# A long-convolution layer on one core: sequences side by side in the spectra's rows, inverse transforms in pairs, and a new order of the engines in the last stage

## The reference, cut to what matters

```
proj = (layernorm(x) @ in_proj_w + in_proj_b).reshape(B, L, C, 3)
v = short_conv(proj[..., 0]) + short_b
h = (gelu(gelu(pos @ fw1 + fb1) @ fw2 + fb2) @ fw3 + fb3)[..., 1]
conv = irfft(rfft(v, 2 * L) * rfft(h, 2 * L), 2 * L)[:, :L]
x = x + (proj[..., 2] * conv) @ out_w + out_b
x = x + layernorm(x) @ (sum_k weights[k] * W[ids[k]]).T + sum_k weights[k] * b[ids[k]]
```

## Time and profile before

| what | value |
|---|---|
| time, median of 3 runs | 2471.45 us (2469.3 to 2475.01) |
| time of the profiled execution | 2469.04 us |
| its span | 2467.2 us |
| PE busy | 2342.2 us, 95% of the span |
| DVE busy | 1555.0 us, 63% |
| POOL busy | 913.5 us, 37% |
| ACT busy | 845.4 us, 34% |
| DMA | 207925 packets, 496.59 MB, mean 201 GB/s |

### The profile page before, as it was taken

The page is one execution under the profiler, slowest core; times in us unless marked ns, Lnnn a source line. Parts: engine busy times, 40 slices in busy tenths (PEclk is TensorE's granted clock), DMA queues, the critical chain, the costliest instruction groups (busy, mean ns, idle before and its releaser), DMA issues. The chain is left out here.

```text
span 2467.2 us, 39561 instructions
## 1 busy us (share of the span) xinstructions
PE 2342.2 (95%) x12804; PEld 1580.8 (64%) x12804; DVE 1555.0 (63%) x2188; ACT 845.4 (34%) x1151; POOL 913.5 (37%) x1189
## 2 busy tenths in 40 slices
PE   7689999999999999779999978999999999999998
PEld 2267777877787777433333326777777777777776
DVE  5834444344444434357767757888888888888886
ACT  3334444444444444234444442222222222222222
POOL 1322222222222222000000006666666666666664
PEclk9889999999999999889999989999999999999999
DMA  5534544544454554689999987655555555555553
GB/s 181 213 98 155 199 138 165 184 177 157 140 195 145 174 169 181 253 310 339 347 333 340 346 298 246 215 171 174 175 173 173 175 173 170 170 174 175 173 176 99
DMA packets 207925, 496.59 MB, mean 201 GB/s; under 512 B 18411, under 2 KB 18732, under 8 KB 190836
## 3 DMA queue, kind: packets, MB, share of 16 engines
q1 hardware_dynamic: 153588, 395.09, 49.8%
q10 hardware_dynamic: 54272, 100.68, 11.1%
HBM read 276.27 MB, written 219.43 MB: 201 GB/s over the span
## 5 line engine op out<-in xcount | busy, mean ns | idle before, releaser
L1052 DVE TENSOR_TENSOR m_m<-m_psA,m_spec 128x1024 f32<-128x1024 f32 x256 | 295.4, 1216 | 149.6 <-PE m_psA L957 146.1
L1212 ACT ACTIVATE b_z<-b_y,b_shift,b_rstd 128x512 f32<-128x512 f32 x128 | 104.5, 816 | 713.3 <-POOL b_shift L1179 703.4
L707 POOL TENSOR_TENSOR vl<-v,vh 128x512 fp32r<-128x512 f32 x128 | 165.2, 1290 | 390.1 <-ACT vh L661 390.1
L974 PE MATMUL m_psW<-m_m,mats 64*64 64x512 f32 x2048 | 248.7, 592 | 0.0
L957 PE MATMUL m_psA<-m_xin,mats 64*64 64x512 f32 x1536 | 203.5, 605 | 43.4 <-DMA m_xin<-spec 36.4
L180 PE MATMUL b_psF<-wfh,b_zh 128*128 128x512 f32 x512 | 214.6, 419 | 3.5 <-DVE b_zl L1315 3.5
L180 PE MATMUL psV<-wvh,nth 128*128 128x512 f32 x512 | 213.6, 417 | 0.6 <-DVE ntl L789 0.6
L180 PE MATMUL b_psO<-woh,b_oh 128*128 128x512 f32 x512 | 211.1, 412 | 0.0
L808 DVE TENSOR_TENSOR gto<-psG,bgr 128x512 f32<-128x512 f32 x128 | 87.7, 685 | 195.3 <-PE psG L182 195.1
L181 PE MATMUL psV<-wvl,nth 128*128 128x512 f32 x512 | 201.0, 393 | 0.0
L182 PE MATMUL b_psF<-wfh,b_zl 128*128 128x512 f32 x512 | 200.9, 392 | 0.0
(11 more groups left out here) (122 smaller groups left out, 4537.5 us busy)
## 6 DMA issues: line engine op xcount, KB each, us to landing
m_xin<-spec SPq DMA_DIRECT2D x31, 2304.0 KB, 14.7
spec<-fs1o SPq DMA_DIRECT2D x32, 2048.0 KB, 10.6
spec<-m_wo ACTq DMA_DIRECT2D x64, 1024.0 KB, 9.8
b_fin<-spec SPq DMA_DIRECT2D x128, 512.0 KB, 3.9
xg<-in_L_attn_x_dram SPq DMA_DIRECT2D x64, 512.0 KB, 6.2
gate_d<-gto SPq DMA_DIRECT2D x32, 1024.0 KB, 3.9
b_gin<-gate_d SPq DMA_DIRECT2D x128, 256.0 KB, 4.1
b_xin<-in_L_attn_x_dram SPq DMA_DIRECT2D x256, 128.0 KB, 3.5
```

The costliest lines, as they stand in the source:

```text
L707: pool.tensor_tensor(vl[:, t % 2], v[:, t % 2], vh[:, t % 2].bitcast(F32), ALU.subtract).then_inc(v_lo, 1)
L974: mm = pe.matmul(psW[pair % 2][half[slot], q, :], ws[slot][half[q]], m[half[q], pair % RM, part, slot, :], start=part == 0, stop=part == 1)
L1052: dve.tensor_tensor(m[:, (k - 2) % RM, part], psA[k % RA][:], spec[:, par, part], ALU.mult).then_inc(m_done, 1)
L1212: act.activation(z[:, t % 2], y[:, t % 2], ACT.Identity, bias=shift[:, t % 2:t % 2 + 1], scale=rstd[:, t % 2:t % 2 + 1]).then_inc(z_done, 1)
```

## The change

- **Layout.** `spec1` and `spec3` change from [sequence, row, channel] to [row, sequence, channel], so that the 8 sequences' pieces of a row, 2 KB each, lie side by side: 16 KB. The filter gets a tensor of its own, `spec_f`.
- **Stores of the front stage.** The four tiles of a store no longer adjoin. The store becomes two DMAs, one for each half h, of 2 KB pieces at a distance of 16 KB; the waits on `s_stored` count 32 for 16.
- **Middle stage.** A group's load becomes two DMAs: the filter (2 KB per row) and the data (16 KB per row). A store has 8 KB per row where it had four pieces of 2 KB.
- **Last stage.** `b_fin` is loaded in pieces of 2 KB at a distance of 256 KB (before: 32 KB). `conv` of an even tile now stands directly ahead of that of the odd tile after it (`conv_pair`, lag 0, where `conv` had lag 1). The lists of TensorE, VectorE, ScalarE and GpSimd get a new order.

```diff
-    spec1 = nc.dram_tensor("spec1", [GB, ROWS * N2, C], F32, kind="Internal").ap()
-    spec3 = nc.dram_tensor("spec3", [B, ROWS * N2, C], F32, kind="Internal").ap()
+    spec1 = nc.dram_tensor("spec1", [ROWS * N2, B, C], F32, kind="Internal").ap()
+    spec_f = nc.dram_tensor("spec_f", [ROWS * N2, C], F32, kind="Internal").ap()
+    spec3 = nc.dram_tensor("spec3", [ROWS * N2, B, C], F32, kind="Internal").ap()
...
-                    sp.dma_start(spec1[b].rearrange("(r h t) c -> r h t c", h=2, t=T)[:, :, t - SUB + 1:t + 1, :],
-                                 s1o[:, slot]).then_inc(s_stored[slot], 16)
+                    rows = spec1.rearrange("(r h t) b c -> b h r t c", h=2, t=T)[b]
+                    for h in range(2):
+                        sp.dma_start(rows[h, :, t - SUB + 1:t + 1, :], s1o[:, slot, h]).then_inc(s_stored[slot], 16)
...
-                by_group = spec_dram.rearrange("b (g p) c -> g p b c", p=P)
                 if isinstance(g, int):
-                    return by_group[g]
-                return by_group[bass.ds(g, 1)].rearrange("g p b c -> (g p) b c")
+                    return spec_dram[g * P:(g + 1) * P]
+                return spec_dram[bass.ds(g * P, P)]
...
-                    sp.dma_start(xin[:, par], rows_of(spec1, group(i, s))).then_inc(x_in[par], 16)
+                    sp.dma_start(xin[:, par, B], rows_of(spec_f, group(i, s))).then_inc(x_in[par], 16)
+                    sp.dma_start(xin[:, par, 0:B], rows_of(spec1, group(i, s))).then_inc(x_in[par], 16)
...
-                            pe.wait_ge(x_in[par], 16 * (i + par))
+                            pe.wait_ge(x_in[par], 32 * (i + par))
...
-                    sp.dma_start(fin[:, t % 2], spec3[b].rearrange("(r h t) c -> t r h c", h=2, t=T)[t]).then_inc(f_in[t % 2], 16)
+                    sp.dma_start(fin[:, t % 2], spec3.rearrange("(r h t) b c -> b t r h c", h=2, t=T)[b, t]).then_inc(f_in[t % 2], 16)
...
-                pipelined(pool, B, T, [(scalars, 3), (bias_y, 3), (correct, 0)])
+                pipelined(pool, B, T, [(correct, 0), (scalars, 3), (bias_y, 3)])
...
-                pipelined(act, B, T, [(norm, 3), (o_high, 1), (z_high, 4), (store, 6)])
+                pipelined(act, B, T, [(z_high, 4), (o_high, 1), (norm, 3), (store, 6)])
...
+                def conv_pair(b, t):
+
+                    if t % 2:
+                        conv(b, t - 1)
+                        conv(b, t)
...
-                pipelined(pe, B, T, [(conv, 1), (adapt, 5), (turn_o, 1), (turn_z, 4), (project, 2)])
+                pipelined(pe, B, T, [(conv_pair, 0), (adapt, 5), (turn_z, 4), (turn_o, 1), (project, 2)])
...
-                pipelined(dve, B, T, [(residual, 3), (gate, 1), (finish, 5), (o_low, 1), (z_low, 4), (bias_x, 0)])
+                pipelined(dve, B, T, [(gate, 1), (residual, 3), (z_low, 4), (o_low, 1), (finish, 5), (bias_x, 0)])
```

More of the change, by code:

```diff
@@ L301, in _ @@
                     sp.wait_ge(s1_out, t + 1)
-                    sp.dma_start(spec1[B].rearrange("(r h t) c -> t r h c", h=2, t=T)[t], s1o[:, t % 2]).then_inc(s1_stored[t % 2], 16)
+                    sp.dma_start(spec_f.rearrange("(r h t) c -> t r h c", h=2, t=T)[t], s1o[:, t % 2]).then_inc(s1_stored[t % 2], 16)
                     if t in (3, 6):
@@ L633, in _ @@
                 for slot in range(2):
-                    sp.wait_ge(s_stored[slot], 16 * B * Q // 2)
+                    sp.wait_ge(s_stored[slot], 32 * B * Q // 2)
                     sp.wait_ge(g_stored[slot], 16 * B * Q // 2)
@@ L666, in s_copy @@
                     if t % SUB == 0 and old(b, t, 2 * SUB):
-                        act.wait_ge(s_stored[slot], 16 * (b * (Q // 2) + t // (2 * SUB)))
+                        act.wait_ge(s_stored[slot], 32 * (b * (Q // 2) + t // (2 * SUB)))
                     act.activation(s1o[:, slot, :, t % SUB], psS[t % 2][:], ACT.Copy).then_inc(s_out, 1)
@@ L902, in load @@
                         for k, piece in enumerate(PIECES):
-                            sp.dma_start(xin[:, par, piece], rows_of(spec1, 0)[:, piece]).then_inc(first_in[k], 16)
+                            src = rows_of(spec1, 0)[:, piece] if k else rows_of(spec_f, 0).rearrange("p (b c) -> p b c", b=1)
+                            sp.dma_start(xin[:, par, piece], src).then_inc(first_in[k], 16)
                         return
```

## The result

| what | before | after |
|---|---|---|
| time, median | 2470.43 us (4 runs, 2469.3 to 2475.01) | 2426.73 us (4 runs, 2423.51 to 2431.23) |
| profiled execution, its span | 2469.04, 2467.2 us | 2427.41, 2425.2 us |
| PE busy | 2342.2 us, 95% | 2317.4 us, 96% |
| DMA | 207925 packets, 496.59 MB | 180517 packets, 496.60 MB |

The ratio is 0.9827, with a 95% interval of 0.9811 to 0.9842: 1.7% faster, against a forecast of 2430 us.

What follows compares the result with a forecast made beforehand. Middle stage taken as waiting slightly for loads, last stage as bound by TensorE's own work. Terms -17.7 - 2 + 0.6 - 22.2 = -41.3 us from 2471.45 gave 2430 us; forecast band 2421 to 2440, range 2418 to 2452.

Steps and rivals of the forecast that it cites:

- Pairs of `conv`, -22.2 us: Last stage: a pair enters and leaves the other matmul shape once, 2.07 for 2.42 us, saving 0.35 x 64 = 22.2 us.
- The end for a shorter drain, 25: Last stage: good end of the pairs' saving, 25 us, if the drain of the stage gets shorter too.
- The cover of the new order, nothing: Last stage: reordered work costs nothing; in a step without a pair 0.6 us are left before turn_o.
- `b_fin` late: Last stage, slower rival: b_fin landing from 10.3 us on idles TensorE before pairs; about 2510 us at 12 us; chance 0.04.
- The front stage's last store, +0.6: End of front stage: the last store, not hidden, grows by 0.4 us and part of an issue; 0.6 us lost.
- The start of the middle stage, -2: Ahead of group 2: cheaper transfers shorten TensorE's wait behind the queue; 2 us saved (0 to 3).
- The middle stage, -17.7: Middle stage: cheaper loads and stores fit into TensorE's period, 12.5 us per group for 13.11; 17.7 us saved.
- A middle stage that stays as it is: Middle stage rival: the piece may not be what slows the loads; 2450 us; chance 0.12 (unchanged or nearly).
- a pair that saves nothing: Last stage rival: each conv itself carries the 0.35 us, so pairing gains nothing; 2452 us; chance 0.09.
- The range's lower end: Whole kernel: 2418 us, given as all terms at their good ends.
- The rule that I set aside: Middle stage loads: by the skill's rule on 8 MiB distances their cost would halve, the sum 3 us better.

Runs made afterwards that it cites:

- the pairs in the old orders: Changed kernel with the old lists of VectorE, ScalarE and GpSimd, and TensorE's old list but with two conv in a row every second step; 2481.07 us.
- The last two experiments: Changed kernel with only spec1 in the new layout, timed again: 2426.14 us; then also first_v's loads for sequences 1 to 7 moved to the last stage: 2417.15 us.
- loads padded: Kernel before with two unused rows (4 KB) behind each sequence of spec1 alone; 2453.15 us.
- stores side by side: Changed kernel with only spec3 in the new layout, spec1 laid out as before; 2459.21 us.
- both padded: Kernel before with two unused rows (4 KB) behind each sequence of both spec1 and spec3; 2453.17 us.

## Why the prediction was right, and where it was not

- **Pairs of `conv`, -22.2 us.** Right. 2.07 us was forecast for a pair and 2.07 measured; the pairs alone give 21.1 us. The front stage's rows were the right place to read the price of a change of shape. The end for a shorter drain, 25, is near what the stage gave with its orders (24.5: 22.8 by the period, the rest outside it).
- **The cover of the new order, nothing.** Right, and needed: the pairs in the old orders are slower than the kernel before. The margin was forecast as 0.6 us. It differs from step to step: in the 58 steps without a pair between 1520 and 2380 us it is 0.23 to 1.34 us, with a median of 0.88, and under 0.6 in 21 of them. That no step waited is therefore closer than the 0.6 says. It is also made up otherwise. The timelines of GpSimd, VectorE and TensorE in one step without a pair:

```profile
1803.80 1.62 POOL L1193 TENSOR_TENSOR b_corr<-b_edge,b_corr 128x512 f32<-128x512 f32 x1
```

```profile
1803.11 1.17 DVE L1289 TENSOR_TENSOR b_xin<-b_xin,bor 128x512 f32<-128x512 f32 x1
1804.20 0.68 DVE L1295 TENSOR_TENSOR b_corr<-b_psC,b_corr 128x512 f32<-128x512 f32 x1
1804.91 1.06 DVE L1300 TENSOR_TENSOR b_o<-b_corr,b_gin 128x512 f32<-128x512 f32 x1
```

```profile
1806.82 0.60 PE L1254 MATMUL b_psP<-b_ident,b_o 128*128 128x128 f32 x4
```

  `bias_x` runs 0.6 us into the step (which begins at 1803.66), not 1.0, and `b_o` takes 1.06 us, not 0.69. `b_o` ends at 1805.97, and `turn_o` starts at 1806.82, 0.85 later.
- **`b_fin` late.** It did not happen: the page's median landing is 4.6 us, forecast as 3.9 and harmless up to 10.3.
- **The front stage's last store, +0.6.** Right. The distance between its issue and the middle stage's first DMA grew from 7.72 to 8.30 us (SyncE's timeline, answering to the earlier trace rows); it is 7.72 to 7.75 in the six traces with the old stores of the front stage and 8.28 to 8.31 in the eight with the new ones:

```profile
1014.99 1.00 SPq L616 DMA_DIRECT2D spec<-fs1o  x2
1023.29 0.37 SPq L895 DMA_DIRECT2D mats<-const_mid_dram  x1
```

- **The start of the middle stage, -2.** It was -1.0, inside the range, and no larger than the spread of kernels with the same layout, so it is not shown. I took it as traffic at a price per MB. The last two experiments show what moves it: which queue gets the engines (36.1 to 32.4 us with stores of 2 KB), and how many bytes are queued ahead of the third group's load (32.4 to 24.9).
- **The middle stage, -17.7.** The size was right (-17.2, period 12.43 on average in all groups but the first), and the step that gave it was wrong. That the size came out all the same is luck: once the loads are on time the period is TensorE's own 12.43, whatever made them so. The wrong step was "since the piece is what changes and not the mixture of reads and writes": the price of a load was scaled by that of stores in longer pieces, to 46.7 us per MB, and the sum of transfers, 11.9 us, was compared with TensorE's 12.42. Measured were 48.4 and 38.0, a sum of 12.1. But with the loads padded the sum is (48.2 x 2.36 + 41.3 x 2.10) / 16 = 12.5 us, the pieces are 2 KB, and nothing waits; with the stores side by side it is 12.5 as well, and TensorE waits 18 us in 300. What makes the kernel before wait is the distance of 8 MB between the pieces of a load. The piece's length matters too, but as one queue's against the other's and not as a price: in the changed kernel the 16 KB loads have to stand up to its own 8 KB stores (period 12.97 with padded 2 KB loads beside them, 12.52 with 16 KB).
- **The rivals.** A middle stage that stays as it is would have shown periods of 13.1, and a pair that saves nothing 7.585 us per tile; neither did. The first was nearer than it looked: its reason, that the piece may not be what slows the loads, was true of the kernel before.
- **The range's lower end.** All terms at their good ends (20, 3, 0 and 25) give 2471.45 - 48 = 2423 us, not the 2418 written. The measured median, 2426.73, lies above both.
- **The rule that I set aside.** I wrote that the trace does not bear it out, because the loads moved 180 GB/s. That was a reason against its figure, not against its direction. Padding by 4 KB made the load land 2.6 to 3.2 us earlier. The Trainium skill (DMA: Bandwidth & Descriptors, "Latency and other measured facts") has this: copies whose partitions' rows lie 4 or 8 MiB apart run at half the rate of short distances, and 4 KB more, measured there at 4 MiB, restore it. Here the distance lies between the pieces inside a partition, and the direction agrees. The size, half the rate, is not seen: a load's cost per MB falls by 4% (50.3 to 48.2). Taking it would have moved the forecast by 3 us only, since TensorE's period of 12.43 us catches either.

## What to carry to other kernels

Price a change of matmul shape from two starts in the trace, and save it by putting equal shapes in a row; then find cover for the longer and shorter steps, since without the new order of VectorE the gain was gone and with all orders old the kernel was 0.5% slower than before in one run. Where a double-buffered load is late by 5%, look at each load's landing against its budget, not at the DMA share nor at the median alone: first at the distance between its pieces, for which a few unused rows are the one-line test, then at what the other queue moves in the same time, and at what constants stand in the queue ahead of it that nobody needs yet.

## What the runs showed that was not expected

- Shares of 1.01 with no wait (both padded, loads padded) and of 0.92 with 18.3 us of waits in 300 (stores side by side): the packets' time as a share of the window is no measure of what the loads need.
- Stores in pieces of 8 KB, cheaper by 8% per MB than in pieces of 2 KB, went with a slower middle stage where the loads beside them kept pieces of 2 KB (period 12.97 for 12.51, both with padded loads; the filter's load apart is the other difference).
- VectorE's `b_o`, which reads two operands from SBUF, takes 0.69 us in the old order and 1.12 on average in the new one, where it runs beside GpSimd's `b_corr`; the gate's first operation, one of whose operands is in PSUM, stays at 0.69. The Trainium skill (SBUF — State Buffer, "SBUF: two separate sides") says that a VectorE operation with two SBUF inputs and a GpSimd operation that reads SBUF exclude each other at a shared port. The trace agrees in which operation grows, and in the step shown above `b_o` starts while GpSimd's `b_corr` runs and ends 0.55 us after it. Here the growth was covered, since `turn_o` never had to wait.
